# A sparse graph-attention layer: a later order of finds, split sort semaphores, three list buffers, and separate landing semaphores for gathers, stores and lists

## What is computed

```python
h = relu(layernorm(x))                       # x is 8192 x 256
h = (h @ W.T).reshape(n, 8, 32)              # 8 heads of 32
attn = s_src[:, None, :] + s_dst[None, :, :] + adj[:, :, None] * We + be
attn = softmax(leaky_relu(where(adj > 0, attn, -inf), 0.2), axis=1)
out = x + einsum('ijh,jhd->ihd', attn, h) + relu(layernorm(x)) @ Wr.T + br
```

## Time and profile before

| | |
|---|---|
| time before, median of 3 runs | 2473.1 us (2469.73 to 2473.41) |
| span of the profiled execution | 2707.2 us; no other time of that execution is recorded |
| DVE busy | 2058.7 us, 76% |
| POOL busy | 1627.7 us, 60% |
| ACT busy | 1264.6 us, 47% |
| PE busy | 1104.5 us, 41% |

### The profile page before, as it was taken

How to read it: one execution, slowest core, us unless ns; L and a number is a source line. 1 busy time by engine, 2 the same in 40 slices (tenths; PEclk the granted TensorE clock), 3 DMA queues, 4 the chain that set the end, 5 groups by cost and what they waited for, 6 DMA issues and landing times.

```text
span 2707.2 us, 24949 instructions
## 1 busy us (share of the span) xinstructions
PE 1104.5 (41%) x3781; PEld 826.0 (31%) x3782; DVE 2058.7 (76%) x5510; ACT 1264.6 (47%) x5256; POOL 1627.7 (60%) x1928
## 2 busy tenths in 40 slices
PE   4676003331150237534363336346245344245244
PEld 3554002221140226322152215225134234234123
DVE  5897819983974899757289848989989999997312
ACT  2332002262121336846585556466475464466376
POOL 5444671477265677677537763675774764763774
PEclk9988556665575667666566656666666666666667
DMA  6446752674644676766358764876877787782332
GB/s 151 152 139 212 223 124 81 189 214 120 200 139 141 208 209 192 214 164 189 106 173 251 200 182 152 236 250 194 254 240 226 240 248 232 237 242 55 85 91 57
DMA packets 166650, 488.40 MB, mean 180 GB/s; under 512 B 35744, under 2 KB 54200, under 8 KB 166280
## 3 DMA queue, kind: packets, MB, share of 16 engines
q1 hardware_dynamic: 86088, 278.11, 31.7%
q0 software_dynamic: 80400, 208.74, 29.4%
HBM read 449.88 MB, written 36.83 MB: 180 GB/s over the span
## 4 chain that ended last, share of the span: by engine, by line
DVE 29%; issue 25%; ACT 12%; DMA 12%; POOL 12%; another core or an unknown queue 5%; PE 3%; SPq 1%; POOLq 0%; DVEq 0%; ACTq 0%
ACT arena L1173 10%; POOL arena L596 10%; DVE work L758 8%; DMA arena<-table,arena 7%; DVE work L747 7%; DVE arena L909 2%; DMA out_dram<-w_all,arena 2%; DVE work L804 2%; DVE work L801 2%; DVE work L803 2%; DVE work L800 1%; DMA adj_sb<-in_adj_dram 1%; PE banks L1327 1%; ACT pre L1158 1%
## 5 line engine op out<-in xcount | busy, mean ns | idle before, releaser
L596 POOL DMA_INDIRECT arena<-table,arena x1253 | 1306.0, 1042 | 624.6 <-issue 392.0
L1173 ACT ACTIVATE arena<-arena,prob 128x32 f32<-128x32 f32 x4456 | 1000.4, 308 | 249.5 <-issue 229.4
L1305 PE MATMUL banks<-arena,ident 128*128 128x256 f32 x1392 | 448.3, 495 | 1109.1 <-DVE arena L909 887.1
L1305 PEld LDWEIGHTS banks<-arena,ident 128*128 128x128 f32 x1392 | 350.9, 258 | 1206.1 <-issue 902.5
L747 DVE FIND_INDEX8 work<-work,adj_sb 128x8 uint32<-128x502 f32 (+56 forms) x775 | 670.7, 868 | 0.0
L758 DVE MAX8 work<-adj_sb 128x8 f32<-128x502 f32 (+56 forms) x775 | 659.3, 858 | 0.0
L1311 PE MATMUL banks<-arena,ident 128*128 128x256 f32 x1114 | 381.8, 472 | 376.2 <-remote 255.6
L1168 ACT ACTIVATE prob<-pre 128x120 f32<-128x120 f32 (+21 forms) x67 | 21.7, 323 | 943.2 <-DVE pre L893 710.5
L1311 PEld LDWEIGHTS banks<-arena,ident 128*128 128x128 f32 x1114 | 226.3, 223 | 516.6 <-remote 303.8
L909 DVE TENSOR_TENSOR arena<-arena,prob 128x768 f32<-128x768 f32 (+8 forms) x166 | 200.7, 1258 | 0.0
L1158 ACT ACTIVATE pre<-arena,we_all 128x13 f32<-128x13 f32 (+27 forms) x536 | 170.4, 407 | 51.4 <-DMA arena<-lists 31.6
(11 more groups left out here) (130 smaller groups left out, 1088.0 us busy)
## 6 DMA issues: line engine op xcount, KB each, us to landing
adj_sb<-in_adj_dram SPq DMA_DIRECT2D x505, 512.0 KB, 15.3
arena<-table,arena POOLq DMA_INDIRECT x1253
table<-arena POOLq DMA_DIRECT2D x32, 264.0 KB, 2.6
arena<-in_x_dram SPq DMA_DIRECT2D x32, 256.0 KB, 2.8
resid<-arena POOLq DMA_DIRECT2D x32, 256.0 KB, 2.6
out_dram<-arena POOLq DMA_DIRECT2D x32, 256.0 KB, 2.8
adj_sb<-in_adj_dram SPq DMA_DIRECT2D x1, 1536.0 KB, 22.6
lists<-arena,rank POOLq DMA_INDIRECT x67
```

The source lines that it names most:

```text
L596: pool.indirect_dma_start(gath[:, un.slot(k), :], None, table[:, :], bass.IndirectOffsetOnAxis(ap=rec[:, k, 0:1], axis=0), bounds_check=N ...
L1173: last = s.activation(g, g, ACT.Copy, scale=prob[:, b, k * H + h:k * H + h + 1])
L1305: last = m.matmul(ps_sum[:, u % 2, :], ident[:, :], gath[:, un.slot(k), 0:HD], start=(k == 0), stop=False)
```

## The change

- The order of finds is given by a table of points with a straight line between them (`FOUND`). Unit 0 has four finds instead of three and unit 1 one instead of two. Units 12, 26, 49, 52, 55, 58 and 61 on have none, and the last find moves from unit 54 to unit 60. By the end of unit 14, 26 sources are found instead of 27.
- The last group of 8 becomes two of 4 (K 20, 11, 9, 8 and 18, 11, 9, 7); 1262 slots instead of 1253, still 67 units.
- The dates of the groups follow from `found`. Those that start at units 19 and 27 are placed, dealt and loaded one unit later than before; those at 35, 43 and 51 are placed two units later, and their deal and load both stand after the gathers of the unit right before their first one.
- Three staging and three list buffers (`HOMES`) instead of two of each.
- `act_slots` is 2K/5 for all K: 479 slots for ACT instead of 557. From unit 15 to 54 it has 82 fewer, and DVE 82 more.
- In the scan the index search runs two segments behind the maximum instead of one. In the sort the lo and hi halves have semaphores of their own, so that each instruction waits for the one two before it.
- The indirect DMAs lose their `bounds_check`.
- Gathers rotate over four semaphores of their own, stores over two, deals and list loads over two.

```diff
-LANES = 4
+LANES = {"landed": 4, "stored": 2, "listed": 2}
...
-          (56, (20, 13, 11, 10, 9, 8, 7, 6)))
+          (56, (20, 11, 9, 8)),
+          (60, (18, 11, 9, 7)))
...
-FOUND = (7, 9, 10, 11, 14, 16, 18, 20, 21, 22)
-LEAD = 13
+FOUND = ((0, 8), (1, 9), (2, 10), (3, 11), (4, 14), (5, 16), (6, 18), (7, 20), (11, 24), (40, 51), (48, 59), (60, 67))
+HOMES = 3
...
-        self.act_slots = K // 2 if K < 18 else 10 if K < 20 or K > 38 else 14 if K < 32 else 16
+        self.act_slots = 2 * K // 5
...
-    found = [FOUND[u] if u < len(FOUND) else min(len(sources), u + LEAD) for u in range(len(units))]
+    found = []
+    for u in range(len(units)):
+        (u0, f0), (u1, f1) = next(((a, b) for a, b in zip(FOUND, FOUND[1:]) if a[0] <= u < b[0]), (FOUND[-1], FOUND[-1]))
+        found.append(f0 + (f1 - f0) * (u - u0) // max(1, u1 - u0))
...
-                    if s:
-                        index(s - 1)
+                    if s >= 2:
+                        index(s - 2)
                 if end == so.segs:
+                    index(so.segs - 2)
                     index(so.segs - 1)
...
-                if m:
-                    dve.wait_ge(S["sorted_"], sorted_before[c] + m)
-                if m % 2 == 0:
-                    v.max(sl, kl)
-                    v.max(sh, kh).then_inc(S["sorted_"], 1)
...
+                for keys_of, top, done in ((kl, sl, S["sorted_lo"]), (kh, sh, S["sorted_hi"])):
+                    if m:
+                        dve.wait_ge(done, sorted_before[c] + m - (c if done is S["sorted_lo"] else 0))
+                    if m % 2 == 0:
+                        v.max(top, keys_of).then_inc(done, 1)
+                    else:
+                        v.match_replace(keys_of, top, keys_of, 0.0).then_inc(done, 1)
...
-            def turn(seq):
-
-                if seq >= LANES:
-                    pool.wait_ge(S[f"landed{seq % LANES}"], 16 * (seq // LANES))
-                return S[f"landed{seq % LANES}"]
+            def turn(kind, seq):
+
+                lanes = LANES[kind]
+                if seq >= lanes:
+                    pool.wait_ge(S[f"{kind}{seq % lanes}"], 16 * (seq // lanes))
+                return S[f"{kind}{seq % lanes}"]
...
-                        bass.IndirectOffsetOnAxis(ap=rec[:, k, 0:1], axis=0),
-                        bounds_check=N + PAD - 1, oob_is_err=False).then_inc(lane, 16)
+                        bass.IndirectOffsetOnAxis(ap=rec[:, k, 0:1], axis=0)).then_inc(lane, 16)
...
-                if group.g >= 2:
-                    before = groups[group.g - 2]
-                    landed(pool, units[before.first + before.n - 1].store_seq + (2 if before.t0 is None else 1))
+                if group.g >= HOMES:
+                    before = groups[group.g - HOMES]
+                    arrived(pool, "stored", units[before.first + before.n - 1].store_seq + (2 if before.t0 is None else 1))
```

More of the change, by code:

```diff
@@ L81 @@
 VMAX = 8 * max([n for n, _ in SEGS.values()] + [len(b) - 1 for b in WINDOW_SEGS])
-WIDE = max(len(ks) * (HEAD + 2 * ks[0]) for ks in LISTS)
+WIDES = [max(len(ks) * (HEAD + 2 * ks[0]) for ks in LISTS[i::HOMES]) for i in range(HOMES)]
 VALID = max(len(ks) * ks[0] for ks in LISTS)
@@ L163, in plan @@
     groups[0].deal_seq, groups[0].load_seq = 0, NV
-    at, owner, part_sums, acts, issued = 0, [None] * GSLOTS, 0, 0, NV + 1
+    at, owner, part_sums, acts = 0, [None] * GSLOTS, 0, 0
+    issued = {"landed": 0, "stored": 0, "listed": NV + 1}
     for un in units:
@@ L386, in flagged_tiles, with arrived @@
                             body(eng, t)
-        def landed(eng, seq):
-            for lane in range(LANES):
+        def arrived(eng, kind, seq):
+            lanes = LANES[kind]
+            for lane in range(lanes):
                 if seq > lane:
-                    eng.wait_ge(S[f"landed{lane}"], 16 * ((seq - lane + LANES - 1) // LANES))
+                    eng.wait_ge(S[f"{kind}{lane}"], 16 * ((seq - lane + lanes - 1) // lanes))
         def record(un):
-            return dealt[:, un.group.g % 2, un.place * un.group.W:(un.place + 1) * un.group.W]
+            return dealt[un.group.g % HOMES][:, un.place * un.group.W:(un.place + 1) * un.group.W]
         def staged(so):
-            return stage[:, so.group.g % 2, so.place * so.group.W:(so.place + 1) * so.group.W]
+            return stage[so.group.g % HOMES][:, so.place * so.group.W:(so.place + 1) * so.group.W]
         def pairs(rec, K):
@@ L405, in listed @@
         def listed(eng, un):
-            landed(eng, un.group.load_seq + 1)
+            arrived(eng, "listed", un.group.load_seq + 1)
         def own_head(group):
@@ L482, in _ @@
                     sp.dma_start(adj_sb[:, b, cols], load_adj(so.t)[:, cols]).then_inc(lane, 16)
-            landed(sp, units[NV - 1].store_seq + 2)
+            arrived(sp, "stored", units[NV - 1].store_seq + 2)
             sp.wait_ge(S["comb_clear"], 2)
@@ L656, in _ @@
                 store(un)
-            landed(pool, issued)
+            for kind, seq in issued.items():
+                arrived(pool, kind, seq)
             pool.wait_ge(S["comb_out"], 16)
@@ L812, in decode @@
                 t, K, rec = so.t, so.K, staged(so)
-                if so.place == 0 and so.group.g >= 2:
-                    before = groups[so.group.g - 2]
-                    landed(dve, before.deal_seq + before.n)
+                if so.place == 0 and so.group.g >= HOMES:
+                    before = groups[so.group.g - HOMES]
+                    arrived(dve, "listed", before.deal_seq + before.n)
                 pv = pairs(rec, K).bitcast(U32)
-                dve.wait_ge(S["sorted_"], sorted_before[c] + 2 * so.rounds)
+                dve.wait_ge(S["sorted_lo"], sorted_before[c] - c + 2 * so.rounds - 1)
+                dve.wait_ge(S["sorted_hi"], sorted_before[c] + 2 * so.rounds)
                 v.tensor_scalar(pv[:, :, 0], slot_lo[:, 0:K], JBITS, None, ALU.logical_shift_right)
```

81 lines of the change are left out of this document (39 added, 42 removed).

## The result

In one measurement, each time beside the kernel before on the same chip, the kernel after took 2486.65 us median (5 runs, 2486.19 to 2491.7) against 2473.1 (5 runs, 2466.36 to 2476.31), ratio 1.0064, 95% interval 1.0051 to 1.0078. On another occasion it was 1.0047 (1.0029 to 1.0064). The forecast was 2488, 0.6% slower. The total came out; whether it did so for the reasons given is the question of the rest.

A forecast was written before the change was run, and what follows sets the result against it. DVE was taken to set the pace in units 15 to 54, POOL's gathers the end and units 4 to 14. The terms, -114 at the end against mostly losses before, summed to +15.5 on 2473.1: 2488 us, range 2415 to 2550.

The forecast's parts named there:

- The end: Stage behind the last find: 107 us after the change instead of 221, since finds fill the idle end; -114 us.
- 20.5 + 31 + 24 + 11: DVE's added work: one more find 20.5, units 55 to 61 31, 82 slots from ACT 24, counting and placing groups 11.
- 82 in place of 22: Hand-overs of a group's list: DVE arrives before the first gathers and waits 82 us, before 22; +60, bounds 47 to 74.
- its term of +12: DVE waiting for PE's ranks at the group at 59 and, shorter, at the last group; +12 us.
- Bounds check: Gathers without bounds check: 0.04 us less each on some 535 gathers on the path; -21 us, bounds 0 to -160.
- The rival that the bounds check decides: Gathers get faster without bounds check: at 0.12 us each -64 us, 2446 us in all; chance 0.27.
- The order: Moving finds into the idle end: end, extra find, seven units, counts, rank waits, ACT waits and hand-overs together; +23.5 us.
- small waits for ACT behind units without a find: +3: In units without a find DVE waits only a little for ACT; +3 us.
- Semaphores: Gathers no longer share their four with stores, -3 us; deals have only two and wait for earlier deals, +4 us.
- the hand-overs don't bind: Rival: POOL gets lists early enough or DVE fills its wait; +60 becomes about -10, 2420 to 2430 us; chance 0.13.
- deals wait for every landing: Rival: on two semaphores each of 60 deals costs 1.1 to 1.6 us, +65 to +95, about 2540 us; chance 0.10.
- The parts cancel within 0.2%: Rival: gains and losses balance, so the time stays within 0.2%, about 5 us; chance 0.12.

The follow-up runs named there:

- the order that keeps the lead: Kernel after with four semaphores for deals and list loads, finds as before up to unit 46, last eight over units 47 to 60: 2395.86 us, ratio 0.968.
- the variant: Kernel after with the order of finds and the groups of the kernel before, everything else of the change kept: 2433.45 us, ratio 0.9812.

## Why the prediction was right, and where it was not

By stage it holds. *The end*: -114 forecast, -109 measured, and the 107 us that were worked out for the new end stage are the 107 measured; the difference is that the old one was 216 and not 221. *The long stage*: its terms 20.5, 31, 24, 11, 12, 3 and 60 sum to 161.5, less some 8 us for bounds and semaphores that fall there; 162 measured. *Up to unit 14*: the rest of the terms, about -24; -40 measured. The account "won at the end, paid back in units 15 to 61" is shown by the windows, and by the order that keeps the lead: with it the stage is 1145 us long instead of 1217, and the end is as it was.

Inside the long stage, kernel before (profiled again) against kernel after: the work came to +76 where 20.5 + 31 + 24 + 11 = 86.5 was forecast. The waits for gathers came to 90.3 us against 30.7, **+60, as forecast** (82 in place of 22); with the 13.4 us on ACT the hand-overs are +73. One part of the 22 was misread: the 9.8 us of the earlier trace rows is a wait for PE's ranks and not for a list. That wait was thus in the stage already (9.3 us before, 10.5 after), and its term of +12 should have been +1. The waits for exponentials rose by 23, 13.4 of them in the hand-overs and 10 behind units without a find, where +3 was forecast.

Among the changes taken one by one, two were far off, the bounds check and the order, with opposite signs. That the total came out within 2 us is luck.

*Bounds check*: -21 forecast, -61 to -65 in the new kernel, -53 in the old one. The 0.04 us was nearly right (0.052). The "535 gathers on the path" was not: 61 to 65 us at 0.052 are some 1200 gathers, nearly all of the 1262. The count left out units 0 to 4, and took a delay in the hand-overs as the gathers' own only. There it seems to be passed on: a list that is later makes the gathers of the next units late, and the exponentials behind them; this is argued from where the waits rose and not shown. The rival that the bounds check decides had the mechanism. Its -64 is the effect that was measured, but from a price twice too high (0.12) times a count half too low; and it was wrong in what was left beside it: without this gain the kernel is 77 us slower than before, not 36.5.

*The order*: +23.5 forecast, 58 to 62 measured by the ratios and 48 by the profiles. The profiled execution of the variant is its slowest, 5 us above its median, and the kernel before took 9 us more on its chip (2481.9 us) than beside the kernel after (2473.1); with these two, 48 becomes 62. Old order to new, both in the new kernel: the end gains 102 and not 114, since with the faster gathers the old end is 209 and not 221. In the long stage DVE's waits for gathers go from 24 to 90 us, +66 where +60 was forecast; that for PE's ranks from none to 10.5 (forecast 12); those for exponentials from none to 25.2, where 3 was forecast. DVE's work there rises by 56 (forecast 62.5). Up to unit 14 the new order wins 9 us that stood in no term; some 4 of them can be the difference of the chips. The step that failed is "small waits for ACT behind units without a find: +3". In these units ACT has still to work off the slots of the one before, as was forecast, but that is 11.8 us. The other 13.4 us were in no term, and with the 66 they make the hand-overs +79, not +60: the hand-over of a list was followed on POOL and DVE alone, and it also goes through ACT, which prepares the new list's first unit before it makes the exponentials of the last unit of the old one. With the lead kept, this second part is gone.

*Semaphores*: -3 and +4 forecast, together +10 to +14 measured, out of +24 to +28 for two list semaphores and -14 for the gathers' own. For the deals the prediction had the right row. But 1.6 us a deal was too much: between first and last deal two semaphores cost 29 us in all, 0.4 a deal, and 7.7 in the two groups at 7 and 11 for which 19 was the upper bound and +4 was taken. What was missing were the other nine groups. The +4 lay between an estimate from the Trainium skill's page "DMA: Bandwidth & Descriptors", section "Anatomy of one DMA — SWDGE (gpsimd) path" (2.1 us to land, no cost) and this row. The page of the kernel after has the median time from issue to landing (the number behind the count is us):

```profile
arena<-table,arena POOLq DMA_INDIRECT x1262, 3.8
...
lists<-arena,rank POOLq DMA_INDIRECT x67, 2.9
```

Against an issue each 1.26 us two semaphores cover 2.5 us. The page's fit lies below this median, and the row decides.

*Slots*: +24 forecast, 7 to 11 measured; DVE's weighting did rise by 23 us in busy time (200.7 to 224.0), but with ACT's slots of before most of that comes back as waits for ACT. *Sort*: -12 forecast, -9 to -14.

The single effects against the kernel after (order 58 to 62, lists 24 to 28, slots 7 to 11; against them bounds 61 to 65, sort 9 to 14, gathers' own semaphores 14) sum to between -4 and +17, by which of its two measurements they are taken from; +12 to +16 was measured. With the first measurement of the kernel after they add up to within 2 us, with the second to within 16. The third staging and list buffers were not run alone, so that they cost nothing is not shown.

Of the marks named: unit 61's evacuation 107 us before the end, yes; waits of 10 us and more at units 27, 35, 43, 51, 52, yes; no wait of 20 us for exponentials, yes (the longest is 11.0 us, at unit 62); 0.20 us or so between the starts of the sort, yes, 0.185 and 0.176 us at 112 elements where they were 0.195 and 0.294; a gather still at 1.00 us, no, its pitch is 1.25 us, just above the 1.24 named as the limit. Deals 2 us and more apart, 13 of 56.

Of the other rivals, "the hand-overs don't bind" is refuted by the 90 us of waits for gathers, and "deals wait for every landing" by the 22 of 67 that do: it was right that two semaphores cost more than +4, and wrong by three in the size. "The parts cancel within 0.2%" missed by little: the lower ends of the two intervals are +0.51% and +0.29%.

## What to carry to other kernels

Before work is moved later to fill an idle end, look at what hangs on it: a chain of ranks, deals, load and gathers has a length of its own (59 us here), and its input must be early by that length; keep the lead where lists are handed over and spread only the last finds, whose lists are the last. Follow the hand-over through every engine that reads the list, in the order of its program: ACT prepared a unit ahead, and so held back work that was ready. Compare stages in an undisturbed profile, and price a change per instruction with all instructions that stand before a late one, not with those at which a wait is seen. When a pool of semaphores is split, each part needs as many as its transfers take in issue intervals to land; here the rare transfers got two, which was too few, and four were enough; three was not run.

## What the runs showed of the hardware

An indirect DMA of 128 rows of 1 KB keeps POOL busy 0.998 us with a bounds check and 0.947 without; the 0.30 us before it is the same in both. Deals, indirect writes issued 1.26 us apart, were still waited for two issues later in 22 cases of 67, with a gap of 4.3 us in the longest against the usual 0.30; with four semaphores in none. Of two sort steps on 312 elements, each waiting for the one right before, the starts lay 1.94 us apart, and 1.69 when each waits for the one two before. A profiled execution can be slower than another of the same program by 235 us (2707.2 against 2471.9 us span), with a small activation each 1.40 us in such a stretch instead of each 0.213; DVE's waits for ACT were 65.6 us in it and 2.0 in the next.
